# Routed expert tiles of a decoder layer: weights stationary in the first product, gated columns written already turned, tile loads issued from another queue

## The reference

```python
x = _layernorm(x + attention(x, qkv_weights))                 # causal, 16 heads
x = _layernorm(x + retention(x, ctx, Wq, Wk, Wv))             # rotary queries and keys, decay mask
hs = x @ sw1 + sb1;  shared = silu(hs[:, :256]) * hs[:, 256:] @ sw2 + sb2
probs = softmax(x @ gate_w + gate_b);  top2 of 8 experts
hr_e = x @ rw1[e] + rb1[e];  out_e = silu(hr_e[:, :256]) * hr_e[:, 256:] @ rw2[e] + rb2[e]
x = _layernorm(x + shared + sum over the two experts of prob_e * out_e)
```

## Time and profile before

| | |
|---|---|
| median of 3 runs | 767.11 us (762.58 to 775.45) |
| the profiled execution | 767.07 us, of which the span of the trace is 765.0 us |
| routed tiles in it | 473.2 to 705.3 us, 71 tiles |
| PE busy over the span | 704.2 us (92%) |
| granted TensorE clock, mean | 0.979 |

### The profile page before, as it was taken

One profiled execution on the slowest core, in us unless ns is written; L12 is line 12 of the kernel. 1 busy time (PEld: TensorE's weight loads), 2 busy tenths in 40 slices (PEclk: granted clock), 3 DMA queues, 4 the chain that ended last, 5 costly groups with the idle time before them and its releaser, 6 DMA issues.

```text
span 765.0 us, 19153 instructions
## 1 busy us (share of the span) xinstructions
PE 704.2 (92%) x5464; PEld 531.8 (70%) x5465; DVE 476.4 (62%) x1435; ACT 449.7 (59%) x1242; POOL 375.1 (49%) x524
## 2 busy tenths in 40 slices
PE   6977899899999999999997897899999999999973
PEld 5866788788888888888875554556565556665542
DVE  2545588788888889888866545344444444443575
ACT  0267788788888888888862221445444444453225
POOL 1001134235445545544545471577777777777212
PEclk9998999999999999999999999999999999999987
DMA  8743564523233323323454257545555555554963
GB/s 292 259 150 105 188 220 146 196 64 93 71 86 91 76 86 100 111 78 102 123 157 160 72 195 205 131 82 86 85 83 88 84 83 83 83 88 59 300 228 138
DMA packets 84778, 97.97 MB, mean 128 GB/s; under 512 B 12160, under 2 KB 76288, under 8 KB 83680
## 3 DMA queue, kind: packets, MB, share of 16 engines
q1 hardware_dynamic: 59728, 64.03, 27.5%
q0 software_dynamic: 14752, 23.53, 15.6%
q10 hardware_dynamic: 10224, 9.49, 4.7%
HBM read 55.90 MB, written 41.10 MB: 127 GB/s over the span
## 4 chain that ended last, share of the span: by engine, by line
PE 66%; DMA 7%; DVE 7%; issue 7%; SPq 6%; POOL 4%; ACT 2%; ACTq 1%; POOLq 0%; DVEq 0%
PE ps L1014 12%; PE ps L1023 6%; PE ps L777 6%; PE ps L874 4%; PE ps L765 4%; PE ps L742 4%; PE ps L787 4%; PE ps L745 3%; PE ps L898 3%; PE ps L877 3%; POOL total L666 3%; PE ps L817 3%; DMA attn_only<-in_ctx 2%; PE ps L1000 2%; PE ps L797 2%
## 5 line engine op out<-in xcount | busy, mean ns | idle before, releaser
L1089 ACT ACTIVATE prob<-ps,nmax 128x128 f32<-128x128 f32 x512 | 146.9, 379 | 29.6 <-DVE nmax L1288 29.6
L1014 PE MATMUL ps<-first_use,xgT 128*128 x284 | 133.8, 593 | 1.5 <-ACT xgT L1207 1.5
L666 POOL DMA_INDIRECT total<-rot,result_row x71 | 112.1, 1579 | 14.1 <-issue 12.8
L1549 DVE TENSOR_TENSOR tile_parts<-ps,attn_only 128x512 f32<-128x512 f32 x71 | 49.1, 692 | 90.0 <-PE ps L1014 90.0
L1288 DVE TENSOR_REDUCE nmax<-ps 128x4 f32<-128x512 f32 x128 | 82.2, 685 | 23.7 <-PE ps L765 22.7
L599 POOL TENSOR_TENSOR rot<-products 128x128 f32<-128x128 f32 x128 | 61.1, 498 | 64.9 <-DVE products L1298 64.7
L1096 ACT COPY pT<-ps 128x512 f32<-128x512 f32 x128 | 76.9, 601 | 20.6 <-PE ps L777 14.4
L777 PE MATMUL ps<-tf,prob 128*128 128x128 f32 x512 | 80.0, 280 | 6.1 <-ACT pT L1096 6.1
L623 POOL DMA_INDIRECT sent<-packets,pos x64 | 63.4, 990 | 36.9 <-PE ps L765 22.6
L1014 PEld LDWEIGHTS ps<-first_use,xgT 128*128 128x128 f32 x284 | 53.5, 190 | 40.1 <-issue 36.5
L650 POOL TENSOR_TENSOR tile_parts<-tile_parts 128x256 f32<-128x256 f32 x71 | 51.1, 720 | 57.2 <-ACT tile_parts L1202 57.2
(11 more groups left out here) (140 smaller groups left out, 1443.2 us busy)
## 6 DMA issues: line engine op xcount, KB each, us to landing
xg<-sent ACTq DMA_DIRECT2D x68, 130.5 KB, 2.1
first_use<-total SPq DMA_DIRECT2D x12, 512.0 KB, 8.6
total<-zeros POOLq DMA_DIRECT2D x1, 4224.0 KB, 17.9
k_dram<-first_use SPq DMA_DIRECT2D x4, 1024.0 KB, 4.4
attn_only<-in_x_turned SPq DMA_DIRECT2D x32, 128.0 KB, 3.2
attn_only<-k_dram SPq DMA_DIRECT2D x256, 16.0 KB
attn_only<-in_x SPq DMA_DIRECT2D x32, 128.0 KB, 2.9
attn_only<-in_ctx SPq DMA_DIRECT2D x32, 128.0 KB, 2.8
```

The source lines that it names most:

```text
L666: eng.indirect_dma_start(totals[slot % 2], bass.IndirectOffsetOnAxis(ap=result_row[:, slot:slot + 1], axis=0), yw[:, slot % 4, :], None, c ...
L1014: mm = eng.matmul(ps[:, r, :], xgT[:, r, c, :], rw1_sb[:, bass.ds(e * (DC * 2 * FFN) + c * 2 * FFN, 2 * FFN)], start=(c == 0), stop=(c == ...
L1089: ins = eng.activation(prob[:, t % 2, 4 * u + n, :], SCORE[u][:, n * P:(n + 1) * P], ACT.Exp, bias=nmax[:, t % 2, 4 * u + n:4 * u + n + 1])
L1549: eng.tensor_tensor(hid[:, r, :], ps[:, r, :], rb_h[:, bass.ds(e * (2 * FFN), 2 * FFN)], ALU.add).then_inc(hid_set, 1)
```

## The change

The tile's expert weights of the first product become the stationary operand and the turned rows move: 8 products with 128 columns in place of 2 with 512. The hidden values so come out with the hidden index on the partitions, the bias is one number per partition, and the gated values are already turned for the second product. So `turn_h`, `out_h`, `product` and `biased` go. New are copies of the first weights from `rw1_sb` at the tile's expert into a fixed place `w_now` (ACT copies one half, `weights_first`, DVE the other, `weights_second`), the tile's bias (`bias_of`) and `gated` on DVE, in two halves, beside two silus. The loads of the packets move from ACT to SP, and 4 of them are interleaved with the loads of the turned rows for the last stage. `result` is now one tile behind instead of two, `result_row` has 4 slots instead of 8, all loops have 4 tiles. The eight loads of `rb1` spread over the partitions go; one small load takes their place at the start. `sgh` gets memory of its own.

```diff
-        rb_h = attn_only[:, 0:BH]
+        w_now = attn_only[:, 0:2 * DC * 2 * FFN].rearrange("p (r c f) -> p r c f", r=2, c=DC)
...
-        result_row = sb("result_row", [P, 8], U32)
+        result_row = sb("result_row", [P, 4], U32)
...
-        tile_parts = sb("tile_parts", [P, 2 * 4 * FFN])
-        hid = tile_parts[:, 0:4 * FFN].rearrange("p (r f) -> p r f", r=2)
-        sil = tile_parts[:, 4 * FFN:6 * FFN].rearrange("p (r f) -> p r f", r=2)
-        gate_h = tile_parts[:, 6 * FFN:8 * FFN].rearrange("p (r f) -> p r f", r=2)
+        sil = attn_only[:, 2 * DC * 2 * FFN:2 * DC * 2 * FFN + 2 * FFN].rearrange("p (r f t) -> p r f t", r=2, f=FFN // P)
+        bias_now = sb("bias_now", [P, 2, 2 * FFN // P])
...
-        sgh = tile_parts[:, :].rearrange("p (q f t) -> p q f t", q=2, f=FFN // P)
+        sgh = sb("sgh", [P, 2, FFN // P, QB * P])
...
+                eng.dma_start(rb1_sb[:, :], rb1).then_inc(small_in, 16)
...
+            def load(i, slot):
+                after(eng, xg_turned, i - 3)
+                after(eng, packet_row, i - 3)
+                after(eng, weight_set, i - 3)
+                row = eng.value_load(tile_row[0:1, bass.ds(i, 1)], min_val=0, max_val=XROWS - P)
+                eng.dma_start(xg[:, slot, :], sent[bass.ds(row, P), :]).then_inc(xg_in[slot], 16)
+
+            load(3, 3)
+            for i in range(4, 8):
+                load(i, i % 4)
+                eng.wait_ge(shid_made, 2 * (i - 4) + 2)
+                load_turned(EARLY + i - 4)
+            with eng.Fori(2, TILES // 4) as k:
+                for n in range(4):
+                    load(4 * k + n, n)
+            for i in range(TILES // 4 * 4, TILES):
+                load(i, i % 4)
...
-            def product(i, r):
-                eng.wait_ge(sil_set, i + 1)
-                after(eng, gh_turned, i - 1)
-                eng.tensor_tensor(gate_h[:, r, :], hid[:, r, FFN:2 * FFN], sil[:, r, :], ALU.mult).then_inc(gh_set, 1)
...
+            def tiles(k, many=4):
+
+                for n in range(many):
+                    i = 4 * k + n
+                    wait_rows(i, n % 2, 2 * k + n // 2)
+                    tile_weight(i + 2, (n + 2) % 4)
+                    add_rows(n)
+
...
-            XGT = ps[:, 2, 0:D]
-            GHT = ps[:, 3, 0:FFN]
+            XGT = ps[:, 7, 0:D]
...
-            def turn_h(i, r):
-                eng.wait_ge(gh_set, i + 1)
-                after(eng, ghT_set, i)
-                for c in range(FFN // P):
-                    mm = eng.transpose(GHT[:, c * P:(c + 1) * P], gate_h[:, r, c * P:(c + 1) * P], ident)
-                mm.then_inc(gh_turned, 1)
-
-            def hidden(i, r, e):
+            def hidden(i, r):
+
                 eng.wait_ge(xgT_set, i + 1)
-                after(eng, hid_set, i - 1)
-                for c in range(DC):
-                    mm = eng.matmul(ps[:, r, :], xgT[:, r, c, :],
-                                    rw1_sb[:, bass.ds(e * (DC * 2 * FFN) + c * 2 * FFN, 2 * FFN)],
-                                    start=(c == 0), stop=(c == DC - 1))
-                mm.then_inc(hid_made, 1)
+                eng.wait_ge(w_first_set, i + 1)
+                eng.wait_ge(w_second_set, i + 1)
+                after(eng, gh_set, 2 * i - 2)
+                for half in range(2):
+                    for f in range(FFN // P):
+                        cols = half * FFN + f * P
+                        for c in range(DC):
+                            mm = eng.matmul(ps[:, 2 * r + half, f * P:(f + 1) * P],
+                                            w_now[:, r, c, cols:cols + P],
+                                            xgT[:, r, c, :], start=(c == 0), stop=(c == DC - 1))
+                    mm.then_inc(hid_made, 1)
 
             def result(i, r, e):
-                eng.wait_ge(ghT_set, i + 1)
+                eng.wait_ge(gh_set, 2 * i + 2)
                 after(eng, yg_set, i - 1)
                 for c in range(FFN // P):
...
-                        turn_h(i - 1, (n - 1) % 2)
-                    if not (first and n < 2):
-                        result(i - 2, n % 2, read[n - 2])
+                        result(i - 1, (n - 1) % 2, before)
                     if not ends:
-                        hidden(i + 1, (n + 1) % 2, read[n + 1])
+                        hidden(i + 1, (n + 1) % 2)
 
...
-            result(TILES - 2, TILES % 2, two_before)
-            eng.wait_ge(sgh_set, 2 * EARLY)
+            last_expert = expert(TILES - 1)
+
+            eng.wait_ge(xgT_set, TILES)
             shared_half(EARLY, 0, 0, 6)
-            turn_h(TILES - 1, (TILES - 1) % 2)
-            result(TILES - 1, (TILES - 1) % 2, before)
             shared_half(EARLY, 0, 1, 6)
-            eng.wait_ge(hid_set, TILES)
+            result(TILES - 1, (TILES - 1) % 2, last_expert)
...
-            def first_row(i):
-                return eng.value_load(tile_row[0:1, bass.ds(i, 1)], min_val=0, max_val=XROWS - P)
-
-            def load(i, slot):
-                after(eng, xg_turned, i - 3)
-                after(eng, packet_row, i - 3)
-                after(eng, weight_set, i - 3)
-                eng.dma_start(xg[:, slot, :], sent[bass.ds(first_row(i), P), :]).then_inc(xg_in[slot], 16)
-
-            def silu(i, r):
-                eng.wait_ge(hid_set, i + 1)
-                after(eng, gh_set, i - 1)
-                eng.activation(sil[:, r, :], hid[:, r, 0:FFN], ACT.Silu).then_inc(sil_set, 1)
+            def silu(i, r, f):
+                if f == 0:
+                    eng.wait_ge(hid_made, 2 * i + 1)
+                    eng.wait_ge(bias_set, i + 1)
+                    after(eng, gh_set, 2 * i - 2)
+                eng.activation(sil[:, r, f, :], ps[:, 2 * r, f * P:(f + 1) * P], ACT.Silu,
+                               bias=bias_now[:, r, f:f + 1]).then_inc(sil_set, 1)
 
             def out_x(i, r):
                 eng.wait_ge(xg_turned, i + 1)
-                after(eng, hid_made, i - 1)
-                eng.copy(xgT[:, r, :, :].rearrange("p c t -> p (c t)"), ps[:, 2, 0:D]).then_inc(xgT_set, 1)
-
-            def out_h(i, r):
-                eng.wait_ge(gh_turned, i + 1)
-                after(eng, yg_made, i - 1)
-                eng.copy(ghT[:, r, :, :].rearrange("p c t -> p (c t)"), ps[:, 3, 0:FFN]).then_inc(ghT_set, 1)
+                after(eng, hid_made, 2 * i - 2)
+                eng.copy(xgT[:, r, :, :].rearrange("p c t -> p (c t)"), ps[:, 7, 0:D]).then_inc(xgT_set, 1)
+
+            def expert(i):
+                return eng.value_load(tile_expert[0:1, bass.ds(i, 1)], min_val=0, max_val=NE - 1)
+
+            def weights_first(i, r, e):
+
+                after(eng, hid_made, 2 * i - 2)
+                eng.copy(w_now[:, r, 0, :], rw1_sb[:, bass.ds(e * (DC * 2 * FFN), 2 * FFN)]).then_inc(w_first_set, 1)
...
-                after(eng, row_added[r], 16 * (added - 1))
+                after(eng, row_added[r], 16 * added)
...
-            def tiles(k, many=8):
-                first, last = isinstance(k, int) and k == 0, isinstance(k, int) and k > 0
+            def tiles(k, many=4):
+                first, last = isinstance(k, int) and k == 0, isinstance(k, int) and k == TILES // 4
                 for n in range(many):
-                    i = 8 * k + n
-                    if not (last and n == many - 1):
+                    i = 4 * k + n
+                    ends = last and n == many - 1
+                    silu(i, n % 2, 0)
+                    silu(i, n % 2, 1)
+                    if not ends:
                         out_x(i + 1, (n + 1) % 2)
-                    silu(i, n % 2)
-                    if not (first and n == 0):
-                        out_h(i - 1, (n - 1) % 2)
+                    if not last or n + 2 < many:
+                        weights_first(i + 2, n % 2, expert(i + 2))
                     if not (first and n < 2):
-                        weighted(i - 2, n % 2, (n - 2) % 4, 4 * k + (n - 2) // 2)
-                    if not (last and n + 3 >= many):
-                        load(i + 3, (n + 3) % 4)
-
+                        weighted(i - 2, n % 2, (n - 2) % 4, 2 * k + n // 2 - 2)
...
-            def biased(i, r, e):
-
-                eng.wait_ge(hid_made, i + 1)
-                after(eng, gh_set, i - 1)
-                eng.tensor_tensor(hid[:, r, :], ps[:, r, :], rb_h[:, bass.ds(e * (2 * FFN), 2 * FFN)], ALU.add).then_inc(hid_set, 1)
+            eng.wait_ge(rb_in, 16)
+
+            def bias_of(i, r, e):
+                after(eng, sil_set, 2 * i - 2)
+                eng.tensor_copy(bias_now[:, r, :], rb1_sb[:, bass.ds(e * (2 * FFN // P), 2 * FFN // P)]).then_inc(bias_set, 1)
+
+            def weights_second(i, r, e):
+                after(eng, hid_made, 2 * i - 2)
+                eng.tensor_copy(w_now[:, r, 1, :], rw1_sb[:, bass.ds(e * (DC * 2 * FFN) + 2 * FFN, 2 * FFN)]
+                                ).then_inc(w_second_set, 1)
+
+            def gated(i, r, f):
+
+                eng.wait_ge(sil_set, 2 * i + f + 1)
```

(61 more changed lines are left out.)

74 lines of the change are left out of this document (26 added, 48 removed).

## The result

The changed kernel takes 801.12 us (median; 795.46 to 803.51), against 769.38 for the kernel before on the same chip: a ratio of 1.044, interval 1.037 to 1.050. One of the six runs of the kernel before took 4014 us; without it their median is 767.11. The ratio leaves out this run and one of 775.45 us, which fell in a slower state; the means compared are 800.4 and 766.8. It is slower, as forecast, by about 33 us where 24 were forecast, so the median lies 10 us above the forecast of 791. The profiled execution took 799.16 us, its span is 797.0, against 767.07 and 765.0.

A forecast was written before the change was run, and what follows sets the result against it. TensorE bounds the kernel before, busy 190.2 of 193 us; after the change a ring of waits would, at 3.5 us a tile. Stage +24.9, end -1.7, start +0.5 on 767.1 gives 790.8, say 791 us; range 764 to 806.

The forecast's parts named there:

- TensorE's part: TensorE's own pass per tile: turn_h goes, hidden takes 16 passes of 128 columns; 2.86 us, 0.16 less.
- The ring: Waits from turn_x over ScalarE, addition, landing and VectorE's weight copy to hidden: 10.25 us for three tiles, 3.42 each.
- long tile: VectorE's tile at the loop's turn, with two more register reads and a branch: 4.15 us.
- VectorE's own walk: VectorE's work per tile: 2.94 us, mean of four 3.3; with the ring 3.42 to 3.60, taken as 3.5.
- The rest: Engines, loads, start and end outside the ring: 512 KB transfers cost nothing, end -1.7 us, start +0.5.
- Start: Ahead of the stage: the small rb1_sb load is one more issue on SP's queue, +0.5 us.
- End: From the last turn_x to the last addition: 10.3 us where it was 12.0, so -1.7.
- The gap of like size: First pass: first out_x now behind two silus, a new gap about as large as the two early load stalls.
- The shared port: VectorE's SBUF-to-SBUF weight copy and GpSimd's descriptor work might lock each other out; evidence was mixed.
- rival (c): weights_second runs into the addition's POOL instruction: 0.6 us more in the ring, 3.7 a tile, 805 us; chance 0.13.
- Rival (a): TensorE stays the bound: a pass of 2.95 us with the loop's turn, 752 us; chance 0.15.
- Rival (b): VectorE's queue reads the register ahead while the row copy waits: 3.2 us a tile, 770 us; chance 0.17.

The follow-up runs named there:

- e1: The changed kernel with eight result_row slots again, VectorE's and GpSimd's loops taking eight tiles: 747.36 us, ratio 0.972 to the kernel before.
- e8: e1 with the row loads back on ScalarE, behind weighted, in place of SyncE: 753.79 us, ratio 0.981 to the kernel before.
- e11: e1 with the row copy waiting for the addition six tiles back in place of eight: 758.83 us, ratio 0.981 to the kernel before.
- e6: The changed kernel, four slots kept, with the row copy moved from VectorE to GpSimd: 752.63 us, ratio 0.980 to the kernel before.
- e7: The changed kernel, four slots, with weighted ahead of weights_first and its register read on ScalarE: 778.92 us, ratio 1.016 to the kernel before.
- e4: The kernel before with four result_row slots in place of eight, nothing else changed: 797.41 us, ratio 1.042 to the kernel before.
- e3: The changed kernel, four slots, with weights_second and its register read ahead of the row copy on VectorE: 784.27 us, ratio 1.014 to the kernel before.
- e5: The changed kernel with the four 512 KB transfers issued behind the loads of tiles 10, 15, 20 and 25: 800.78 us, ratio 1.047 to the kernel before.
- e2: e1 without re-reading two registers in the middle of VectorE's loop of eight: 752.75 us, ratio 0.980 to the kernel before.

## Why the prediction was right, step by step

- **TensorE's part** held. A pass without a wait is 2.87 (forecast 2.86), hidden 534.09 - 532.31 = 1.78 (forecast 1.78), and the gain of a shorter pass is there in e1: 11.7 us less stage than before, 3 to 4 of it from the early loads (e8), the rest from the pass. Behind a wait hidden takes 1.88.
- **The ring** was the right mechanism, shown twice: with more slots (e1, e11) or with the wait on another engine (e6) the loss goes. That its path goes over ScalarE to the addition is shown by e7. Terms: landing 3.88 (3.8), landing to the copy of weights 0.98 (0.95), the copy 0.43 (0.55), out_x to weights_first 0.78 (0.85), weights_first 0.62 (0.62), weighted 0.51, start of weighted to the addition 0.51 + 0.80 (0.51 + 0.60), hidden 1.88 (1.78). From the addition at 609.54 to the one at 620.02, a ring with no loop turn in it, are 10.48 us for three tiles, against 10.25. The ring over four tiles that the chain shows, 14.73 us, is that one with VectorE's long tile in it, which the prediction had as 4.15 + 10.25 = 14.40: from one copy of weights to the next the long tile took 4.17 (607.03 to 611.20).
- What failed in it is a sentence of reason: "nothing that TensorE needs stood behind it" in the kernel before. The next tile's biased did; only the eight slots kept the wait from binding (e4). The share that the interleaved copy of weights has in the loss is the smaller one: putting it ahead gives back 17 us of 48 (e3).
- **VectorE's own walk**: the mis-sized term, 3.5 us a tile where 3.64 were measured. I had 3.42 to 3.60 a tile and took 3.5, "since part of the long tile is also part of a ring". The loop turn is wholly in the ring: silu waits for bias_of, which stands behind the two reads, so rings over the turn take 602.16 to 613.53 = 11.37 us. So the bound that I had as the upper one, 3.60, was the better price. The steady mean is 3.64 (64 passes, without the first five and the long one): 64 x 0.14 = 9.0 us more.
- **The rest**: the 512 KB transfers between the loads were set at "nothing". For the loads that held; for the additions it didn't. One landed late and one pass took 8.88, 5.4 more than 3.5; 1.7 of that is the lower granted clock (3.57 in place of 1.88). Against that the first five passes, before the ring closes, took 14.2 in place of 17.5: -3.3. The sum is 9.0 + 5.4 - 3.3 = 11.1, the stage's 256.1 less 245. "Start" was +0.5 and measured -2.3 (470.99 against 473.24); but the first turn_x of runs that change nothing ahead of the stage came anywhere from 466.26 (e5) to 480.15 us (e11), so one execution does not measure this term, and its sign here is luck. "End" was -1.7 and measured -2.2 (9.8 us); the stretch after it was 0.4 longer. 790.8 + 11.1 - 2.8 - 0.5 + 0.4 + 0.1 (outside the span) = 799.1, the profiled time is 799.16. This sum fits the one profiled execution; the runs of the changed kernel spread from 795.5 to 803.5. The gap of like size in the first passes that I set against the early loads wasn't there: they took 2.76 to 2.87.
- **The shared port**, rival (c): hardly a sign of it. In e1, 55 of 61 copies of weights from 500 to 690 us overlapped an addition's GpSimd instruction and took 0.44 us on average (the longest 0.63), the other 6 took 0.43, and in the changed kernel it was 0.46 against 0.43, 27 and 26 copies. The Trainium skill ("SBUF — State Buffer", "Who interferes with whom") has the two lock each other out for a whole instruction; here, some hundredths on average and 0.2 us at most. The estimate by its figures for the faster mode, 0.42, was the better price: the copy took 0.43, mine was 0.55.
- **Rival (a)** was the state of the kernel with the ring cut: 752 forecast, 747 to 753 measured in e1, e2 and e6, and its condition, "additions would have to be issued or land much earlier", is what more slots amount to. **Rival (b)** fell: the read of the register starts at 606.19, 0.12 us after the late row copy had started (606.07), and not ahead of it.

## What to carry to other kernels

When a ring of buffers is shortened, look for the engine on which its wait stands, and list everything behind it in that queue up to the one that frees the buffer: if the list closes a ring, its length over the number of tiles that it spans is a bound on the pass (14.73 over four and 10.48 over three here, 7.11 over two in e4). Here four slots of four bytes a partition were worth more than the whole rearrangement, 47.7 us of stage against 11.7: with eight slots or the wait that six would have, or the row copy on the engine that waits for the landing anyway, the same change is 2 to 3% faster than the kernel before, in place of 4.4% slower. A step at a loop's turn is to be added to such a ring in full until a trace shows it hidden.

## What the runs showed of the hardware

- A register read on VectorE that follows a waiting instruction doesn't overlap that wait: 0.30 + 0.19 us in the chain. At a loop's turn two reads and the branch took 1.6 us (607.42 to 609.02).
- After TensorE had waited 4.06 us its granted clock was at the 1.2 GHz level from 490 to 494 us; in e1, where the engine was busy all of 480 to 500 us, the granted clock stayed at 1.00 (0.83 in the changed kernel). In e8 a wait of 1.98 us was followed by a granted clock of 0.57 from 485 to 489 us.
- 16 passes of hidden take 1.78 us when TensorE comes to them without a pause and 1.88 after even a short wait.
- An indirect addition of 128 rows lands in 3.8 us at the median (3.7 to 3.9 in the kernel before, 3.6 to 4.4 in e4), whatever the pass; with 512 KB transfers beside it the one at 482.52 took some 6.4 us, and three in e5 took 5.7 to 5.9.
- Copies of 128 x 512 f32 on VectorE from SBUF to SBUF took 0.43 us, and 0.44 on average where an addition's GpSimd instruction ran beside them (e1).
